# A language-model layer on one core: the first LayerNorm's gathers in one row, five of its roots on VectorE, its normalisation on ScalarE, and zero matmuls in between

## The reference

```python
h = take(W.T, x)                                  # x: 4 x 512 token numbers, rows of 128 floats
h = h + attn(layernorm(h))                        # attn: s = tanh(s @ A.T + x_t @ B.T), step by step over 512
                                                  # positions; then C, a sigmoid gate, Wo
h = h + ffn(layernorm(h))                         # ffn: 8 experts, each row goes to its best one, and a shared
                                                  # expert for all rows
def layernorm(x): return (x - mean(x)) / sqrt(var(x) + 1e-5)
```

## Time and profile before

| | us |
|---|---|
| median of 3 runs | 182.01 (180.23 to 183.34) |
| the profiled execution | 182.58 |
| its span on the core | 180.7 |
| PE busy | 138.5 (77%) |
| DVE busy | 127.2 (70%) |
| ACT busy | 104.7 (58%) |
| POOL busy | 84.1 (47%) |

### The profile page before, as it was taken

One profiled execution on the slowest core, in us unless ns is written; L12 is line 12 of the kernel. 1 busy time (PEld: TensorE's weight loads), 2 busy tenths in 40 slices (PEclk: granted clock), 3 DMA queues, 4 the chain that ended last, 5 costly groups with the idle time before them and its releaser, 6 DMA issues.

```text
span 180.7 us, 3231 instructions
## 1 busy us (share of the span) xinstructions
PE 138.5 (77%) x997; PEld 99.7 (55%) x997; DVE 127.2 (70%) x365; ACT 104.7 (58%) x239; POOL 84.1 (47%) x77
## 2 busy tenths in 40 slices
PE   0105997788898888886799988899939989999720
PEld 0104864666675666675445878466726657666510
DVE  1245676927499995999779899488825778887730
ACT  2001444589989983587779993675532645655400
POOL 3768874900000000343100658552687787886580
PEclk9999999969999999999999999999996999999995
DMA  4564345899000000012200033410122443433331
GB/s 153 150 184 138 97 140 195 278 384 365 7 0 0 4 0 4 2 60 95 79 4 0 29 91 114 134 32 16 47 45 31 45 42 33 44 33 34 29 33 15
DMA packets 9955, 14.37 MB, mean 80 GB/s; under 512 B 1936, under 2 KB 4624, under 8 KB 9936
## 3 DMA queue, kind: packets, MB, share of 16 engines
q1 hardware_dynamic: 5904, 10.45, 16.9%
q0 software_dynamic: 4032, 3.67, 13.3%
HBM read 10.71 MB, written 3.41 MB: 78 GB/s over the span
## 4 chain that ended last, share of the span: by engine, by line
DMA 22%; PE 20%; POOL 18%; DVE 14%; ACT 12%; issue 10%; POOLq 1%; SPq 1%; DVEq 0%
DMA w_sb<-x_rows,row_in 7%; PE bank L655 6%; POOL w_sb L415 6%; POOL emb_rows L371 5%; DMA emb_rows<-emb,tok_sb 5%; POOL out L422 4%; PE bank L680 4%; DMA xblk<-x_rows,row_in 4%; ACT attn_out L725 4%; DMA w_sb<-w 3%; ACT states L702 3%; ACT w_hl L742 3%; PE bank L478 2%; PE bank L668 2%; DMA out<-w_sb,row_of 2%
## 5 line engine op out<-in xcount | busy, mean ns | idle before, releaser
L422 POOL DMA_INDIRECT out<-w_sb,row_of x20 | 31.3, 1564 | 9.1 <-DVE w_sb L1205 4.8
L478 PE MATMUL bank<-states,sq_sb 128*128 128x128 f32 x108 | 27.1, 335 | 6.0 <-ACT states L702 1.6
L655 PE MATMUL bank<-w_hl,xblk_t 128*128 x120 | 30.4, 391 | 1.0 <-issue 1.0
L403 POOL TENSOR_TENSOR rstd<-vareps,cst 128x2 f32<-128x2 f32 x8 | 5.7, 710 | 45.7 <-DVE vareps L853 45.7
L478 PEld LDWEIGHTS bank<-states,sq_sb 128*128 128x128 f32 x108 | 17.4, 202 | 14.2 <-ACT states L702 13.8
L812 ACT ACTIVATE w_sb<-bank,factor 128x512 f32<-128x512 f32 x20 | 13.8, 688 | 19.4 <-PE bank L655 19.3
L476 PE MATMUL bank<-x_in,sq_sb 128*128 128x128 f32 x108 | 23.3, 299 | 1.6 <-ACT x_in L695 1.5
L415 POOL DMA_INDIRECT w_sb<-x_rows,row_in x16 | 17.5, 1094 | 12.4 <-issue 6.3
L702 ACT ACTIVATE states<-bank 128x128 f32<-128x128 f32 x54 | 14.9, 276 | 12.2 <-PE bank L478 12.0
L680 PE MATMUL bank<-w_hl,w_sb 128*128 x160 | 16.6, 246 | 5.7 <-DVE w_sb L1205 5.7
L476 PEld LDWEIGHTS bank<-x_in,sq_sb 128*128 128x128 f32 x108 | 17.9, 207 | 2.8 <-ACT x_in L695 1.6
(11 more groups left out here) (160 smaller groups left out, 288.9 us busy)
## 6 DMA issues: line engine op xcount, KB each, us to landing
w_sb<-w SPq DMA_DIRECT2D x24, 256.0 KB, 6.4
x_rows<-norm SPq DMA_DIRECT2D x4, 256.0 KB, 2.4
out<-attn_out SPq DMA_DIRECT2D x4, 256.0 KB, 3.1
late<-places SPq DMA_DIRECT2D x1, 619.5 KB, 8.3
sw_sb<-sw SPq DMA_DIRECT2D x2, 256.0 KB, 3.0
cst<-consts SPq DMA_DIRECT2D x1, 420.0 KB, 3.3
sq_sb<-sq SPq DMA_DIRECT2D x1, 384.0 KB, 3.7
out<-w_sb,row_of POOLq DMA_INDIRECT x20, 3.3
```

Source lines behind the costliest of these rows:

```text
L422: pool.indirect_dma_start(out=out, out_offset=bass.IndirectOffsetOnAxis(ap=row_of[:, k:k + 1], axis=0), in_=out_blk[k % RING], in_offset=N ...
L478: pe.matmul(pre, at, states[:, i * COLS:(i + 1) * COLS], start=False, stop=True).then_inc(pre_ready, 1)
L655: mm = pe.matmul(hb[:], xblk_t[:, k % 3, b * P:(b + 1) * P], w[:, bass.ds(e * INNER + a * EXPERTS * INNER, INNER)], start=(j == 0), stop=( ...
```

## The change

- All sixteen gathers stand in one row at the start of POOL's program. Ahead of them POOL does one power of a single value.
- The last pair is taken apart: its two tiles have semaphores of their own (`gathered[7]`, `gathered_last`), moments, root, norm, turn and bring.
- The roots of the pairs 0 to 4 (`OWN_ROOTS`) are taken on DVE by `own_root`: a first value from the bits, and two Heron steps, with three reciprocals in all. It also writes a shift, minus mean times root.
- The norms of these five pairs are taken on ACT (`norm_own`), one ACTIVATE a tile, after the steps 0, 2, 4 and 6 (pair 0 ahead of step 0). Their order against the tanh of each step is fixed by ACT's program.
- The pairs 5 and 6 and the two tiles of pair 7 keep the root on POOL (`late_root`, after all gathers) and the norm on DVE.
- `TURN_AT`: pair n, for n from 1 to 4, was turned after step 2n - 2 and is turned after step 2n - 1. Pair 5 stays after step 8, pair 6 goes from step 11 to 10, and pair 7 from step 13 to 11 (first tile) and 12 (second).
- `hum` issues matmuls of zeros with 512 columns on PE: ten ahead of the first turn, one behind it, one or two after each of the steps 0 to 7, ahead of the turn that stands there.
- The first turn and spread of the greatest values stand two steps later. Of the eight 512-column pieces of w1's low half, two stand ahead of the second scales and six behind them; it was three and five.

```diff
-TURN_AT = {0: 1, 2: 2, 4: 3, 6: 4, 8: 5, 11: 6, 13: 7}
-ROOTS = ((0, 1, 2), (3,), (4,), (6,), (7,))
+OWN_ROOTS = 5
+TURN_AT = {1: 1, 3: 2, 5: 3, 7: 4, 8: 5, 10: 6, 11: 7, 12: 8}
+HUM_BEFORE = 10
+HUM = {0: 1, 1: 2, 2: 1, 3: 2, 4: 1, 5: 2, 6: 1, 7: 2}
-MAX_STEPS = (20, 32)
-SPREAD_STEPS = (22, 34)
+MAX_STEPS = (22, 32)
+SPREAD_STEPS = (24, 34)
...
# SyncE
-                if 1 + j < PAIRS:
+                if 1 + j < PAIRS - 1:
                     sp.wait_ge(gathered[1 + j], 32)
+                if 1 + j == PAIRS - 1:
+                    sp.wait_ge(gathered_last, 16)
...
# TensorE
+            def hum(count):
+                for _ in range(count):
+                    pe.matmul(bank[6][:], zeros[:], zeros[:, 0:1].to_broadcast([P, GC]), start=True, stop=True)
+
+            pe.wait_ge(zeros_set, 1)
+            hum(HUM_BEFORE)
             turn_pair(0)
             pe.wait_ge(pads_zero, 1)
+            hum(1)
...
             for i in range(STEPS - 1):
                 advance(i)
-                if i in TURN_AT:
-                    turn_pair(TURN_AT[i])
+                hum(HUM.get(i, 0))
+                n = TURN_AT.get(i, 0)
+                if 0 < n < PAIRS - 1:
+                    turn_pair(n)
+                if n >= PAIRS - 1:
+                    turn_late(n - PAIRS + 1)
...
# ScalarE
+            def norm_own(n):
+
+                act.wait_ge(shift1_ready, n + 1)
+                if n >= 2:
+                    act.wait_ge(norm_turned, n - 1)
+                for i, t in enumerate(pair_tiles(n)):
+                    act.activation(norm_rows[:, n % 2 * 2 + i, :], emb_rows[:, t, :], ACT.Identity,
+                                   bias=shift1[:, t:t + 1], scale=rstd[:, t:t + 1]).then_inc(norm_ready, 1)
...
+                if i % PPP == 0 and i // PPP + 1 < OWN_ROOTS:
+                    norm_own(i // PPP + 1)
...
# VectorE
+            def own_root(n):
+
+                tiles = pair_tiles(n)
+                ts = slice(tiles[0], tiles[1] + 1)
+                dve.wait_ge(gathered[n], 32)
+                moments(tiles)
+                then_wait(dve.tensor_scalar(vareps[:, ts], meanvar[:, ts, 1], EPS, SQRT_C * SQRT_C / 16, ALU.add, ALU.mult))
+                dve.tensor_scalar(quarter[:, ts], meanvar[:, ts, 1], EPS, 0.25, ALU.add, ALU.mult)
+                then_wait(dve.tensor_scalar(root_a[:, ts].bitcast(I32), vareps[:, ts].bitcast(I32), 0.5, float(SQRT_SEED),
+                                            ALU.mult, ALU.add))
+                then_wait(dve.reciprocal(inv_a[:, ts], root_a[:, ts]))
+                for t in tiles:
+                    ins = dve.scalar_tensor_tensor(out=root_b[:, t:t + 1], in0=inv_a[:, t:t + 1], scalar=vareps[:, t:t + 1],
+                                                   in1=root_a[:, t:t + 1], op0=ALU.mult, op1=ALU.add)
+                then_wait(ins)
+                then_wait(dve.reciprocal(inv_b[:, ts], root_b[:, ts]))
...
+                then_wait(dve.reciprocal(rstd[:, ts], root_c[:, ts]))
+                dve.scalar_tensor_tensor(out=shift1[:, ts], in0=meanvar[:, ts, 0], scalar=-1.0, in1=rstd[:, ts],
+                                         op0=ALU.mult, op1=ALU.mult).then_inc(shift1_ready, 1)
...
+            for n in range(OWN_ROOTS):
+                own_root(n)
             dve.wait_ge(wgc_done, 1)
             dve.tensor_copy(wgc[:], bank[4][:, 0:P]).then_inc(wgc_ready, 1)
...
+            dve.wait_ge(gathered[5], 32)
+            late_variance(pair_tiles(5))
+            dve.wait_ge(gathered[6], 32)
+            late_variance(pair_tiles(6))
+            late_normed(5)
+            dve.wait_ge(gathered[PAIRS - 1], 16)
+            late_variance((before_last,))
+            late_normed(6)
...
-            w1_low(slice(0, 2 * INNER))
+            w1_low(slice(0, INNER))
             turned_greatest(1, 2)
-            w1_low(slice(2 * INNER, 3 * INNER))
+            w1_low(slice(INNER, 2 * INNER))
             powers_of_two(1, SECOND)
...
+            w1_low(slice(2 * INNER, 4 * INNER))
             dve.wait_ge(w1_high, EXPERTS // 2)
-            w1_low(slice(3 * INNER, 8 * INNER)).then_inc(w_split, 1)
+            w1_low(slice(4 * INNER, 8 * INNER)).then_inc(w_split, 1)
```

144 lines of the change are left out of this document (74 added, 70 removed).

## The result

The changed kernel takes **191.54 us** (median of 4, 189.57 to 192.22) beside 181.15 us for the kernel before on the same chip (median of 4, 180.23 to 183.34): a ratio of **1.057, 95% interval 1.045 to 1.070**. It is slower by 10 us where 178.3 was forecast. Its profiled execution took 191.14 us, with a span of 189.3; the one of the kernel before took 182.58, with a span of 180.7.

What follows compares the result with a forecast made beforehand. Bound: a chain of waits headed by the first LayerNorm's supply of rows, mostly GpSimd's own program. 182.58 - 3.6 (earlier rows and weights) - 0.9 (clock) + 0.2 (VectorE's tail) = 178.3 us; range 176.2 to 181.2.

Steps and rivals of the forecast that it cites:

- Gathers in a row: GpSimd's row: at 1.24 us a gather, the sixteenth starts at 21.5 and the last landing comes 3.6 us earlier.
- Sixteenth gather at 21.5, parts 3.6 earlier: GpSimd and weights: sixteenth gather at 21.5 instead of 25.24; third weights' part for the squares at 32.5 instead of 36.1.
- `own_root` 2.55, reciprocal 0.17: VectorE: one root of a pair, from moments to shift, takes 2.55 us, each reciprocal 0.17.
- Norms 0.88; zeros 7.1 to 11.6; tanh 0 at 13.2: ScalarE's two norms take 0.88 us; TensorE's first ten zero matmuls run 7.1 to 11.6; first tanh at 13.2, not 17.74.
- The loop at 2.77: Early recurrence: tanh, norms, turn and bring form a loop of 2.77 us for two steps, against 1.7 without waits.
- Tanh 8 at 24.3: Recurrence: step 8's tanh comes at 24.3 us, four turns of 2.77 us behind tanh 0 at 13.2.
- Pair 5 in time for the turn behind step 8: Pair 5's root on POOL ends at 23.2, its norm at 23.8; step 9 then takes 1.2 us instead of 0.85.
- The fall of the clock at 37 goes: Recurrence, steps 18 to 22: TensorE's clock no longer falls to 0.50, worth -0.9 us (bounds 0 and -0.9).
- VectorE's tail, +0.2: VectorE behind the second scales: one more piece of w1's low half costs 0.2 us, between 0 and 0.57.
- The norms on ACT, the roots on DVE and the zeros are worth nothing beyond what makes the row of gathers possible: Recurrence to step 18: early steps gain 4.5 us, the loop eats what exceeds the weights' limit, leaving -3.6 us.
- Rival C: TensorE: zero matmuls don't bring or keep the high clock and stand in the path at 0.45 each; 186.5 us, chance 0.07.
- Rival D: GpSimd's row: gathers slow beside VectorE, each of the last ten 0.15 us longer, losing 1.5 us; 179.8 us, chance 0.06.

Runs made afterwards that it cites:

- e4: Changed kernel with a GpSimd power of six values (1.4 us) behind the eighth and the twelfth gather; 181.17 us beside 180.39 for the kernel before.
- e17: Changed kernel with a short GpSimd power behind each of pairs 1 to 6, six pauses; 187.08 us.
- e16: Changed kernel with GpSimd waiting idle till the eighth and twelfth gathers have landed, timed against the kernel before; 183.23 us, ratio 1.012.
- e2: Changed kernel without any matmuls of zeros; 188.48 us.
- e3: Changed kernel without the power of one value ahead of the gathers; 192.05 us.
- e6: Changed kernel with GpSimd waiting, before each pair from the third on, for the landing of the pair two before; 188.28 us.
- e9: Changed kernel with SyncE issuing no part of the weights before the last landing; 190.80 us.
- e12: Changed kernel with GpSimd waiting idle till the eighth and the twelfth gather have landed, one execution; 183.34 us.
- e10: Changed kernel with two GpSimd pauses of 1.4 us (powers of six values), both behind the fourth gather; 190.03 us.
- e8: Changed kernel with GpSimd drained once, behind the eighth gather; 183.19 us.
- e13: Changed kernel with a 1.4 us power behind the eighth gather, pair 5's root between fourteenth and fifteenth, pair 5 normalised ahead of pair 6's moments; 185.10 us, ratio 1.014.
- e11: Changed kernel with GpSimd drained behind the second and the twelfth gather; 185.27 us.
- e15: Changed kernel with 1.4 us powers behind the eighth and twelfth gathers, timed against the kernel before; 185.06 us, ratio 1.016.
- e5: Changed kernel with one GpSimd power of a single value (0.58 us) behind the eighth gather; 192.97 us.
- e14: Changed kernel with one GpSimd pause of 1.4 us (power of six values) behind the eighth gather; 186.03 us.
- e7: Changed kernel with a GpSimd power of a single value behind the fourth, eighth and twelfth gather; 189.85 us.

## Why the prediction was wrong

**The step that failed is the first: "Gathers in a row".** It read the row's price from the eight gathers that already stood in a row (1.24 us each), and this held for sixteen: 1.25. That the row would cost *other* engines anything was not asked; no rival named it. The kernel before never issued more than eight without 2.4 or 1.6 us of something else behind them (12.52 to 14.96 and 19.80 to 21.42 by the earlier trace rows), so no row of its trace could show it. The runs showed in its place: with the pauses taken out, waits of VectorE and ScalarE end 0.3 to 6 us late from about the tenth gather on, until 1.1 us behind the last landing, and step 2's tanh comes at 27.18 instead of 16.0 by the forecast's loop (13.2 + 2.77).

Point by point:

- *Sixteenth gather at 21.5, parts 3.6 earlier*: right. The gather started at 21.82, and SyncE went on at 24.35 instead of 28.32, 4.0 us earlier (the landing took 2.5 us by this, not 3.18). It was worth nothing, since the recurrence ended last and the weights waited for it, not it for them.
- *`own_root` 2.55, reciprocal 0.17*: right (2.65 and 0.17).
- *Norms 0.88; zeros 7.1 to 11.6; tanh 0 at 13.2*: right (0.88; 6.90 to 11.37; 13.13).
- *The loop at 2.77*: right where nothing was late (2.69). Tanh 8 at 24.3 held in e4 (24.12), e17 (24.35) and e16 (24.64), with the row broken, and failed by 12 us without.
- *Pair 5 in time for the turn behind step 8*: it depended on the row, as POOL takes the root behind the last gather. In e4, whose row ends 2.7 us later, step 9 comes 3.6 us behind step 8 (24.12 to 27.73) instead of the forecast 1.2, and the clock is at 0.50 from 28 to 30 us.
- *The fall of the clock at 37 goes*: it went, but another, at 19.4, came in its place, while TensorE stood idle.
- *VectorE's tail, +0.2*: it can't be made out beside 7.4, and no run isolates it.
- *"The norms on ACT, the roots on DVE and the zeros are worth nothing beyond what makes the row of gathers possible"*: borne out as far as the runs go. With the row broken the kernel is at 1.012 of the kernel before (e16, 0.997 to 1.026), with a last gather 0.65 us later.
- *Rival C* named a slow time (186.5) for another reason: zeros in the path at 1.2 GHz. The zeros didn't stand at 1.2 GHz: the clock was 1.00 up to 19.4 us, and fell while TensorE stood idle, as it had from 14.6 on; e2 without them is nearly as late (tanh 8 at 33.69, here 36.32). It had the sign right and the cause wrong, and even its 186.5 was 5 us short.
- *Rival D* had the row suffer from VectorE. It was the other way round. The gathers kept 0.94 to 0.95 us from the third on, beside VectorE's roots, so the lock between the two that the Trainium skill describes (SBUF — State Buffer, "SBUF: two separate sides") shows nowhere in this row.

**What is settled and what is open.** Shown: without breaks in the row VectorE's waits were late in each run in which that engine was at work beside it (the changed kernel, e2, e3, e6, e9), and with the row broken up and all else kept they were gone (e4, e12, e16, e17). Neither the zeros, nor the probe, nor the weights' traffic makes them. The sum of the pauses isn't all that counts: the sixteenth gather starts 2.7 us later than 21.82 in e4, 3.0 in e17 and 4.1 in e12 and e16, which leave VectorE none; but also 2.6 in e10, 3.1 in e8, 3.8 in e13 and 5.2 in e11, where late waits of one engine or both stayed, and 2.6 in e15, the kernel of e4. The first four have their pauses in at least two places with four gathers between them or fewer; of the others here only e15 has. Smaller sums were too little wherever they stood: 1.0 us in e5, 1.2 in e14, 2.2 in e7, whose three pauses are four gathers apart. The kernel before, with 3.4, has them after the eighth and the twelfth, as e4 and e12. Apart from e4 with e15 and e12 with e16, each of these is one execution.

Not settled is what builds up. It is not gathers that haven't landed (e6), nor the weights' transfers (e9), and no more than 0.7 us of it shows in a drain (e11). The Trainium skill (DMA: Bandwidth & Descriptors, "SWDGE vs HWDGE vs iDMA") says that GpSimd computes the descriptors of its own DMAs and appends them to rings that the DMA engines empty; no run here shows the rings. Nor can I say whether the recording of the trace has a part in it, since every time here comes from a recorded execution.

## What to carry to other kernels

A pause in GpSimd's program that looks like waste can be what keeps the other engines' waits short: before you close up a row of indirect gathers to more than eight, put the closed row alone on the chip, beside engines that are at work, and look at waits of an engine on its own last instruction. When a price is read from a short row, ask what a row twice as long does to everybody else, and give that a rival of its own. If bracketed waits are named "issue" or "remote" on several engines at once, the cause may lie in none of them; look at what the one engine does that isn't waiting.

## What the hardware showed that I had not expected

- Waits that end late through a neighbour's gathers: 0.34 to 1.86 us on VectorE, up to 6.08 on ScalarE in the changed kernel, while the instructions kept their length (a gather 0.94, a reciprocal 0.17, inside and outside of the stretch).
- The late instructions start on a grid of about 0.71 us. In the changed kernel 16.27, 16.99, 17.70, 19.12, 20.52, 21.95, 24.06, 24.78 and 25.49 lie 0.72, 0.71, 1.42, 1.40, 1.43, 2.11, 0.72 and 0.71 apart. Another run agrees, with differences of 0.70 and its multiples: in e2 16.06, 16.76, 18.16, 18.86, 22.39, 23.79, 24.50 and 25.20. ScalarE's late instructions often start with VectorE's, to 0.01 us: 26.06 on both in e5, 26.50 in e7, 21.94 in e11, 27.61 and 27.60 in e10. What beats at that rate I don't know.
- The last late wait of VectorE ends near the last landing, by SyncE's next issue, but not with it: at 25.49 against 24.35 in the changed kernel, 25.38 against 24.33 in e9, 26.06 against 25.73 in e5, 26.50 against 27.29 in e7.
- A drain of GpSimd behind gathers took 2.73, 3.27 and 3.41 us, a mere wait for their landing 2.09 and 2.75 (e12).
